# A two-layer graph network: the values' bias through the last weights, copies swapped between two engines, products turned by token tile

## The reference, cut to what matters

```python
# layer 0: 12 heads of 32
h = einsum('bnd,ade->bane', feat_in, W);  th = tanh(h)
attn = th @ w_src + swap(th @ w_dst);  attn = leaky(attn, 0.2)
attn = softmax(where(mask, -999.0, attn))
feat_out = elu(concat_heads(attn @ h + b))
gate = sigmoid(feat_in @ H_w.T + H_b)
out0 = gate * feat_out + (1.0 - gate) * feat_in
# layer 1: 6 heads of 64
q, k, v = heads(s @ Wq + bq), heads(s @ Wk + bk), heads(s @ Wv + bv)
probs = softmax(q @ k.T / sqrt(64) + where(adj, 0, -9e15))
out1 = concat_heads(probs @ v) @ Wf + bf
```

## Time and profile before

| | |
|---|---|
| median of 3 runs | 1048.03 us (1046.15 to 1048.07) |
| profiled execution, its time | 1046.33 us |
| profiled execution, its span | 1044.4 us, 24816 instructions |
| mean granted TensorE clock | 0.982 of full |
| TensorE, VectorE, ScalarE, GpSimd busy | 93%, 74%, 60%, 26% |

### The profile page before, as it was taken

How to read it: one execution, slowest core, us unless ns; L and a number is a source line. 1 busy time by engine, 2 the same in 40 slices (tenths; PEclk the granted TensorE clock), 3 DMA queues, 4 the chain that set the end, 5 groups by cost and what they waited for, 6 DMA issues and landing times.

```text
span 1044.4 us, 24816 instructions
## 1 busy us (share of the span) xinstructions
PE 968.0 (93%) x10037; PEld 840.1 (80%) x10037; DVE 775.1 (74%) x1456; ACT 630.1 (60%) x1242; POOL 273.4 (26%) x338
## 2 busy tenths in 40 slices
PE   6689999999999999999999999999999999999696
PEld 5487978889797888978788897878879788887575
DVE  4868877777787778868777886877788687877814
ACT  5657576484746757485675747567574755756332
POOL 2223150502415041240504124050421405032110
PEclk9699999999999999999999999999999999999987
DMA  8310151420415143041513405141240414121102
GB/s 233 51 24 11 32 93 32 91 33 32 62 33 93 32 81 44 16 78 33 93 32 74 49 4 92 32 93 32 68 48 11 94 32 93 33 49 23 23 31 62
DMA packets 183797, 56.61 MB, mean 54 GB/s; under 512 B 164994, under 2 KB 183684, under 8 KB 183684
## 3 DMA queue, kind: packets, MB, share of 16 engines
q1 hardware_dynamic: 183684, 55.02, 28.9%
HBM read 17.26 MB, written 12.58 MB: 29 GB/s over the span
## 4 chain that ended last, share of the span: by engine, by line
PE 53%; DVE 25%; issue 9%; ACT 6%; POOL 4%; DMA 1%; SPq 0%; DVEq 0%; ACTq 0%; POOLq 0%
PE ps L661 12%; PE ps L663 11%; PE ps L662 11%; PE ps L647 7%; PE ps L739 5%; PE ps L839 4%; DVE x L1001 4%; DVE ee L998 4%; DVE hT0l L907 3%; DVE hT1l L1096 3%; PE ps L857 3%; ACT p L440 2%; DVE p L1026 2%; DVE mx L1024 2%; PE ps L805 2%
## 5 line engine op out<-in xcount | busy, mean ns | idle before, releaser
L420 POOL TENSOR_TENSOR x_in<-x_in,ee 128x384 f32<-128x384 f32 x64 | 68.5, 1070 | 615.1 <-DVE ee L1004 615.1
L1060 DVE TENSOR_TENSOR hT1l<-ps,hT1h 128x512 fp32r<-128x512 f32 x48 | 30.4, 684 | 93.5 <-ACT hT1h L575 93.4
L647 PE MATMUL ps<-ident,p 128*128 128x128 f32 x576 | 80.4, 285 | 19.3 <-ACT p L440 10.7
L413 POOL TENSOR_TENSOR x_in<-x_in,h 128x384 f32<-128x384 f32 x64 | 85.1, 1359 | 16.4 <-DVE Wf_lo L932 16.4
L1037 DVE COPY_PREDICATED_SCALAR z<-not_adj,masked 128x768 f32 x64 | 69.6, 1087 | 26.3 <-ACT z L528 26.3
L647 PEld LDWEIGHTS ps<-ident,p 128*128 128x128 f32 x576 | 65.5, 145 | 28.1 <-issue 12.5
L661 PE MATMUL ps<-Wf_hi,hT1h 128*128 128x384 f32 x192 | 69.0, 359 | 10.4 <-DVE hT1l L1096 10.4
L491 ACT ACTIVATE ps<-hb_all 128x384 f32<-128x384 f32 x56 | 27.7, 495 | 79.6 <-DVE x_in L1049 79.6
L407 POOL TENSOR_TENSOR x_in<-x_in,bf_row 128x384 f32<-128x384 f32 x64 | 62.4, 1008 | 43.1 <-ACT p L440 43.1
L528 ACT ACTIVATE z<-ps 128x384 f32<-128x384 f32 x128 | 52.5, 498 | 30.9 <-PE ps L739 30.9
L661 PE MATMUL ps<-W_hi,hT0h 128*128 128x384 f32 x192 | 65.4, 341 | 3.5 <-DVE hT0l L907 3.5
(11 more groups left out here) (132 smaller groups left out, 2820.0 us busy)
## 6 DMA issues: line engine op xcount, KB each, us to landing
V<-v_tok SPq DMA_DIRECT2D x128, 192.0 KB, 4.9
x_in<-in_x_dram SPq DMA_DIRECT2D x16, 768.0 KB, 5.0
out_dram<-x_in SPq DMA_DIRECT2D x16, 768.0 KB, 3.5
x<-in_L_gnn_H_w_dram SPq DMA_DIRECT2D x1, 576.0 KB, 5.9
QT<-in_L_gnn_W_dram SPq DMA_DIRECT2D x3, 192.0 KB, 6.7
thT<-in_L_gnn_Wq_dram SPq DMA_DIRECT2D x1, 576.0 KB, 8.1
z<-in_L_gnn_Wk_dram SPq DMA_DIRECT2D x1, 576.0 KB, 8.6
z<-in_L_gnn_Wv_dram SPq DMA_DIRECT2D x1, 576.0 KB, 9.7
```

What stands on the lines that cost most here:

```text
L413: pool.tensor_tensor(x_in[:, i % 3, t], x_in[:, i % 3, t], h0[:, par, t], ALU.add).then_inc(x_plus_h, 1)
L420: pool.tensor_tensor(x_in[:, i % 3, t], x_in[:, i % 3, t], ee[:, t], ALU.subtract).then_inc(x2_made, 1)
L647: return pe.transpose(dst, src, ident[0:rows, 0:rows])
```

## The change

- **Bias.** bv is no longer added to the values. In iteration 0 it is spread over columns (ScalarE), multiplied once by Wf (TensorE) and added to `bf_row` (VectorE).
- **Copies.** Values of layer 1 are copied out of PSUM by ScalarE (`copy_values1`), turned tanh by VectorE.
- **Turning by token tile.** Each bank holds three chunks of one tile (384 columns), four banks a group. High and low parts are made by tile (`high_tile`, `low_tile`). `project` (queries and keys) does the six matmuls with the high right-hand part first. The values of layer 0 and the last product wait by tile.
- **Score blocks.** A half covers one half of the heads for all four tiles, graph in the outer loop. The softmax of layer 0 goes in four units of two tiles by half the heads.
- **Layer 1's attention.** The exponentials are summed and divided in `p1` before they are turned. The attention is then made turned (values stationary, probabilities moving), written to one bank a tile, and goes straight to its high and low parts; the 12 turns of it are gone. `V1` loses its column of ones, and its spread becomes eight transfers of half the size.
- **Order.** Layer 0's attention of tile 2 comes before layer 1's turns, tile 3 before layer 1's attention; h0's turns are split in two pairs of tiles, the first before layer 1's turns. VectorE divides layer 1 first, then layer 0's tiles 0 to 2, and makes the first two h0 remainders ahead of layer 1's.

```diff
@@ RING
-            + jobs("thT_copied", 0, thT_copied, 3)
-            + jobs("h1_low", 1, h1_low, 3)
+            + jobs("thT_copied", 0, thT_copied, 4)
+            + jobs("h1_low", 1, h1_low, 4)
...
-            + jobs("attn0_made", 0, attn0_made, 4)[0:2]
+            + jobs("attn0_made", 0, attn0_made, 4)[0:3]
+            + jobs("h0_low", NEXT, h0_low, 4)[0:2]
             + jobs("probs1T_copied", 1, probs1T_copied, 3)
-            + jobs("attn0_made", 0, attn0_made, 4)[2:3]
-            + jobs("attn1_made", 1, attn1_made, 4)
             + jobs("attn0_made", 0, attn0_made, 4)[3:4]
-            + jobs("h0_low", NEXT, h0_low, 3)
-            + jobs("attn1_low", 1, attn1_low, 3)
+            + jobs("attn1_low", 1, attn1_low, 4)
+            + jobs("h0_low", NEXT, h0_low, 4)[2:4]
             + jobs("out_made", 1, out_made, 4)
@@ SyncE
                     for g in range(2):
-                        for o in range(2):
-                            sp.dma_start(V1[64 * o:64 * o + 64, g].rearrange("p t k e -> p (t k) e")[:, :, 0:E1],
-                                         v_tok[64 * g:64 * g + 64].rearrange("p t (k o e) -> p (t k) o e", o=2, e=E1)[:, :, o])\
-                                .then_inc(values1_spread, 16)
+                        for r in range(2):
+                            for b in range(2):
+                                sp.dma_start(V1[64 * r:64 * r + 64, g, b].rearrange("p q k e -> p (q k) e"),
+                                             v_tok[64 * g:64 * g + 64, 2 * b:2 * b + 2]
+                                             .rearrange("p q (k o e) -> p (q k) o e", o=2, e=E1)[:, :, r ^ b])\
+                                    .then_inc(values1_spread, 16)
@@ ScalarE
+            def high_tile(to, name, t):
+                toks = slice(t * P, (t + 1) * P)
+                return act.activation(to[:, :, toks], ps[:, job(name, t) % BANKS, 0:D].rearrange("p (c m) -> p c m", m=P), ACT.Copy)
...
+                def copy_values1(t):
+                    if real(j):
+                        act.wait_ge(values1_full, TILES * j + t + 1)
+                        if t == 0 and real(i):
+                            act.wait_ge(values0_spread, 64 * (i + 1))
+                        act.activation(v_tok[:, 2 * (t % 2) + t // 2], ps[:, job("values1_made", t) % BANKS, 0:D], ACT.Copy)\
+                            .then_inc(values1_made, 1)
...
+                copy_values1(0)
                 exp0(3)
+                copy_values1(1)
+                copy_values1(2)
+                copy_values1(3)
@@ TensorE
+                def blocks(half_of):
+                    for t in range(TILES):
+                        take(i, job("leaky_made", 4 * half_of + t))
+                    for g in range(2):
+                        for t in range(TILES):
                             rows = slice(SD * t, SD * t + SD)
...
+                    for b in range(2):
+                        take(i, job("attn1_low", 2 * pair + b))
+                    for k in range(PAIRS1):
+                        for b in range(2):
+                            t = 2 * pair + b
+                            q, at = divmod(t * PAIRS1 + k, 4)
                             for o in range(2):
+                                rows = slice(64 * (o ^ b), 64 * (o ^ b) + 64)
                                 for g in range(2):
+                                    mm = pe.matmul(ps[64 * o:64 * o + 64, job("attn1_low", t) % BANKS, k * P + g * N:k * P + (g + 1) * N],
+                                                   V1[rows, g, b, pair, k], KT[rows, q, at * P + g * N:at * P + (g + 1) * N],
+                                                   start=True, stop=True, skip_group_check=True)
...
+                if i == 0:
+                    pe.wait_ge(bv_spread, C)
+                    pe.wait_ge(w_loaded["Wf"], 16)
+                    dst = take(i, job("values1_made", 0))[:, 0:D]
+                    for c in range(C):
+                        mm = pe.matmul(dst, KT[:, c, 0:P], staged["Wf"][:, c], start=(c == 0), stop=(c == C - 1))
+                    mm.then_inc(bv_through, 1)
+                    pe.wait_ge(bf_made, 1)
@@ VectorE
+                def divide1(pair):
                     if real(j):
+                        probs = p1_pair(pair).rearrange("p t (h m) -> p t h m", m=N)
+                        sums = rs1[:, 2 * pair:2 * pair + 2]
+                        dve.wait_ge(probs1_made, TILES * j + 2 * pair + 2)
+                        dve.tensor_reduce(sums, probs, AX_X, ALU.add).then_inc(sums1_made, 1)
+                        dve.wait_ge(sums1_made, 2 * j + pair + 1)
+                        dve.reciprocal(sums, sums).then_inc(inv1_made, 1)
+                        dve.wait_ge(inv1_made, 2 * j + pair + 1)
+                        dve.tensor_tensor(probs, probs, sums.unsqueeze(3).broadcast_to((P, 2, HEADS1, N)), ALU.mult)\
+                            .then_inc(probs1_divided, 1)
...
+                divide1(0)
+                divide1(1)
                 divide0(0)
                 divide0(1)
                 divide0(2)
...
+                if real(i + 1):
+                    h0_lows(i + 1, range(0, 2))
+                if real(j):
+                    for t in range(TILES):
+                        dve.wait_ge(attn1_high, TILES * j + t + 1)
+                        low_tile(hT1l, hT1h, "attn1_low", t).then_inc(attn1_low, 1)
                 divide0(3)
                 if real(i + 1):
+                    h0_lows(i + 1, range(2, 4))
```

More of the change, by code:

```diff
@@ L257, in hw_bank @@
         def hw_bank(c):
-            taken = [job("th_made", t) % BANKS for t in range(TILES - 1)] + [job("h0_low", k) % BANKS for k in range(C)]
+            taken = [job("th_made", t) % BANKS for t in range(TILES - 1)] + [job("h0_low", k) % BANKS for k in range(TILES)]
             return [b for b in range(BANKS) if b not in taken][c - C]
@@ L725, in project @@
                     cols = slice(o * P, (o + 1) * P)
-                    product(ps[:, job(name, o) % BANKS], lambda c: wh[w][:, c, cols], lambda c: wl[w][:, c, cols],
-                            lambda c: hT1h[:, c], lambda c: hT1l[:, c],
-                            chunk_ready=lambda c: (h1_low, C * j + c + 1)).then_inc(full, 1)
-                def blocks(pair):
-                    take(i, job("leaky_made", 4 * pair + 3))
-                    take(i, job("leaky_made", 4 * pair))
-                    take(i, job("leaky_made", 4 * pair + 1))
-                    take(i, job("leaky_made", 4 * pair + 2))
-                    for half_of in range(2):
-                        for t in (2 * pair, 2 * pair + 1):
-                            rows = slice(SD * t, SD * t + SD)
-                            for g in range(2):
-                                mm = pe.matmul(ps[64 * g:64 * g + 64, job("leaky_made", 2 * t + half_of) % BANKS, 0:D],
-                                               src_rows[rows, g * N:(g + 1) * N],
-                                               thT[rows].rearrange("p c m -> p (c m)")[:, (2 * g + half_of) * D:(2 * g + half_of + 1) * D],
-                                               start=True, stop=True, skip_group_check=True)
@@ new lines, in project @@
+                    dst = ps[:, job(name, o) % BANKS]
+                    pe.wait_ge(h1_high, TILES * (j + 1))
+                    for c in range(C):
+                        pe.matmul(dst, wh[w][:, c, cols], hT1h[:, c], start=(c == 0), stop=False)
+                        pe.matmul(dst, wl[w][:, c, cols], hT1h[:, c], start=False, stop=False)
+                    pe.wait_ge(h1_low, TILES * (j + 1))
+                    for c in range(C):
+                        mm = pe.matmul(dst, wh[w][:, c, cols], hT1l[:, c], start=False, stop=(c == C - 1))
@@ new lines, in project @@
+                    mm.then_inc(full, 1)
+                def blocks(half_of):
+                    for t in range(TILES):
+                        take(i, job("leaky_made", 4 * half_of + t))
+                    for g in range(2):
+                        for t in range(TILES):
+                            rows = slice(SD * t, SD * t + SD)
+                            mm = pe.matmul(ps[64 * g:64 * g + 64, job("leaky_made", 4 * half_of + t) % BANKS, 0:D],
+                                           src_rows[rows, g * N:(g + 1) * N],
+                                           thT[rows].rearrange("p c m -> p (c m)")[:, (2 * g + half_of) * D:(2 * g + half_of + 1) * D],
+                                           start=True, stop=True, skip_group_check=True)
@@ L816, in body, with unit_of, pair_of, turn_probs @@
                     scores(1)
-                def turn_probs(name, ready, done, src, pairs, n, jobs):
+                def unit_of(n, t, pair):
+                    return TILES * n + 2 * (pair // PAIRS1) + t // 2 + 1
+                def pair_of(n, t, pair):
+                    return 2 * n + t // 2 + 1
+                def turn_probs(name, ready, made, done, src, pairs, n, jobs):
```

(3 more changed lines are left out.)

256 lines of the change are left out of this document (121 added, 135 removed).

## The result

| | before | changed |
|---|---|---|
| median of 4 runs each | 1047.09 us | 1006.41 us (1006.08 to 1008.23) |
| profiled execution: time, span | 1046.33, 1044.4 | 1006.25, 1004.5 |

The ratio is 0.9612, with a 95% interval of 0.9599 to 0.9625: 40.7 us or 3.9% faster. The forecast was 1004.5 us.

The account below looks back on a forecast made before the run. TensorE was taken to bound almost the whole period. Savings of 1.3 + 1.2 + 0.4 = 2.9 us in each of 15 periods, 43.5 us, set against the 1048.03 us median, gave 1004.5 us; range 996 to 1029.

Parts of the forecast that it names:

- W to Q: Start of the last product (W) to the first query product (Q): 1.3 us gained per period from 24.13.
- Q to S: First query product (Q) to the scores (S), 22.29 us: two score-block calls 0.6 us shorter each, 1.2 together.
- S to W: Scores (S) to the next last product (W): 14.84 us becomes 14.4, the rest turning into waits for VectorE.
- three marks: VectorE's chain in S to W: two divisions to S+9.7, three layer-0 divisions to S+11.9, two h0 remainders to S+12.9.
- Ends: Outside the full periods: group 0 plus 2 us, the last group minus 2 us, together 0.
- Rival 1: Score blocks: eight array places don't run at once, blocks keep 1.45 us; 1022.5 us, chance 0.17.
- Rival 2: Layer 1's attention: two row groups writing one bank are serialised, 1.67 becomes 3.3 us; 1028.5 us, chance 0.12.
- Rival 3: Layer 1's values: the last of eight transfers lands 1.8 us too late; 1031 us, chance 0.07.
- Rival 4: S to W: growing waits make the clock fall to 1.2 GHz; up to 1080 us, chance 0.04.
- Rival 5: Whole period: VectorE becomes the bound, its rows slipping 2.9 us more; near no change, chance 0.05.

Follow-up runs that it names:

- e1: Changed kernel with turned tanh copied by ScalarE again, four copies by tile ahead of those of h1: 1028.4 us.
- e3: Changed kernel with `project` taking its nine matmuls in the old order, all behind VectorE's last remainder: 1021.89 us.
- e11: Changed kernel with VectorE's division of layer 0's fourth tile moved ahead of layer 1's remainders: 1002.48 us.
- e4: Changed kernel with score blocks of tiles 2 and 3 using the rows of tiles 0 and 1, so four array places instead of eight: 1028.1 us.
- e6: Changed kernel without layer 1's division (sums, reciprocal and multiplication left out, a one-column copy signals instead): 986.69 us.
- e8: Changed kernel with the bias row added after the second softmax unit of group 0, not behind the last shift: 1004.65 us.
- e9: The changed kernel run again without any edit: 1007.08 us.
- e5: Changed kernel with score blocks tile by tile, graph in the inner loop, and layer 1's attention rotating through its places: 1006.61 us.
- e7: Changed kernel with GpSimd multiplying the first pair of probabilities and ScalarE's third ELU exponential behind the first half's high parts: 1002.68 us.
- e12: Changed kernel with e7, e8, e11, the attention's order of e5 and layer 1's mask made ahead of the maxima: 987.38 us.

## Why the prediction was right

The forecast (1004.5 us, measured 1006.41) held with its mechanism; sizes were off in small terms. The saving is the stricter measure: 43.5 us forecast, 40.7 measured. Of the difference 0.9 doesn't show in the total, since the median before came down from 1048.03 with three runs to 1047.09 with four.

- **W to Q**, predicted 24.13 to 22.85, measured 22.82. The cause was ScalarE's queue: e1 gives both waits back and e3 one of them. The prediction had the order in `project` only as cover for the last remainder; it is worth 0.87 us a period, since Q would wait for all of ScalarE's and VectorE's work in a row. The stretch isn't quite without waits: the one for a bank in the last product wasn't foreseen (e11 takes 0.34 us back).
- **Q to S**, predicted -1.2, measured -1.13. Two blocks gave 1.24 (0.83 us each, predicted 0.81); 0.11 was lost in the values' product, whose 36 matmuls took 6.45 us instead of 6.34, one every 0.1767 instead of 0.1733. In e4 they go at 0.1733 in ten of 16 groups. Why is open. What the Trainium skill, "TensorE: Matmul & The Clock Gate", "Measured speedup vs the span model", says of sixteen places running together (10.6 times one) no run here shows; the 1.2 us that the prediction drew from it for eight is near the 1.24 measured.
- **S to W**, predicted 14.4, measured 14.61. VectorE's chain came within 0.1 us at each of its three marks. The term that was too small is the attention: 1.89 us where 1.75 was used, behind a third division 0.1 us late; 12.09 + 1.89 + 0.63 for the h0 turns is 14.61. Most of this lies in the wait at its middle, which the prediction put at 0.07 us: VectorE's h0 remainders end at S+12.87 (526.53), and there TensorE's records thin out (windows below, columns as in the earlier trace rows). In e6, where these remainders are done before the attention starts, no quarter of a microsecond inside it has under 28 records, and it takes 1.73, 0.16 less. That the mean of S to W fell by 0.38, next to the 0.4 forecast, is luck: against the steady period that the prediction cut out (14.84) the gain is 0.23, and the rest came because the periods before were longer on average than that one. The foreseen kind of loss, waits for VectorE, is confirmed by e6: without the division the stretch is 1.29 shorter.

```profile
526.25:526.50 0.25, 0.25 (x28) 0.25 (x23) 0.25 (x1) 0.25 (x1) 0.00 (x0) 1.00 0.00 0
526.50:526.75 0.25, 0.25 (x20) 0.24 (x12) 0.03 (x1) 0.03 (x1) 0.00 (x0) 1.00 0.00 0
```

- **Ends**, predicted +2 and -2. Group 0 lost 1.7 us up to the first Q, for the stated reason (e8 takes 2.0 back). The last group gained 1.1, but its -2 isn't shown: in e9's trace of the same kernel it takes 67.5 us from W to the end, 0.6 more than before, and of the kernel before there is one trace. The sum also used 15 full periods; 14 lie between the first W and the one that begins the last iteration, and ahead of the first W there is no W to Q that could gain. The -0.66 at the ends plus 39.2 make 39.9 us of span where 43.5 was forecast: 1.4 from 2.80 instead of 2.9 a period in 14, and 2.2 from the ends (a 15th period's 2.9 was counted, 0.66 came).
- **Rival 1** (eight places don't run at once) is excluded by e4. **Rival 2** (attention serialised) by 1.89 us for 96 instructions, 1.79 in e5, where 3.3 was its price. The rule of the Trainium skill, "TensorEngine Tiling (Array Packing)", "Gotcha 1: PSUM Pressure", that different row tiles can't access one bank at the same time, cost no time here with the two row groups on different partitions of the bank; the measurement decides. What row groups on the same partitions do wasn't tried.
- **Rival 3** (values late): SyncE's timeline shows the eight transfers issued by S+6.95, each landing a median 2.4 us later, so about S+9.4; the attention starts at S+12.1. The longest landing, 3.9 us, would make it S+10.9. They cost 0.72 us each to issue, not 0.9, and could be issued from S+1.2 on, not S+2.4: ScalarE was through with the values at S+1.18 (its queue was sized 1.1 us too long).

```profile
514.86 5.75 SPq L365 DMA_DIRECT2D V<-v_tok x8
```

- **Rival 4** (the clock falls): 1.00 in mid-span, S to W included. **Rival 5** (VectorE the bound): it is the bound of two waits in S to W, 1.1 us together, and not of the period, in which it is busy 48.2 of 58.6 us.

Shown by runs are the worth of the tanh swap, of the order in `project`, of eight places and of the division, each alone. The worth of the removed turns of layer 1's attention was not measured alone, nor that of the bias's way and of the new order of h0's turns.

## What to carry to other kernels

Before counting busy shares, cut one period into stretches and ask at each customer which queue is late: here moving 1.5 us of copies to an engine that sat idle at that moment gave 1.4 us a period, while moving 1.6 us of copies between the same two engines where nobody waited gave nothing. Small matmuls gained here by going to more different places of the array next to each other (eight instead of four, e4); which of them comes first hardly mattered here (e5). Where several waits stand in a row, shortening one shows the next (e6, e7), so the edits pay together: e7, e8 and e11 alone bring 4, 2 and 5 us, e12 with these and two smaller ones 20.

## What the runs showed of the hardware that I had not expected

- A GpSimd multiplication of 128x768 takes 1.47 us, and VectorE's multiplication of the same size beside it takes 1.26 us instead of 0.96, though only its first 0.44 us lie beside GpSimd's (520.62 to 521.06 in e7). VectorE's sums of the second pair, beside it but for their first 0.16 us, took 0.89 us, no longer than in the changed kernel (0.95), so not every operation is held up. Each pair of probabilities lies in its own part of memory, so it isn't the data that they share.
- Products of 36 split matmuls that were not edited run at one of two paces, 0.1733 or 0.1767 us a matmul, and the values and gate of layer 0 take the same one in a period. The values' product of layer 1 has the slower pace in none of 16 groups before and in all 16 after the change. Eight places in the blocks ahead of it can't be the whole reason: with four (e4) it has it in 6 of 16, and in the last group, which has no such blocks, one trace of the changed kernel has the slower pace and the other the faster.
- After a thinly busy stretch the return from 1.2 to 2.4 GHz came at different times in executions with the same work: the last group's Q to S took 19.79 and 21.57 us in two traces of the changed kernel, with a mean granted clock of 1.00 and 0.90. Differences of 2 us in this kernel need the mid-span stretches, not the total, to be told apart.
